# A graph network on one core: the edge softmax moves into the first aggregation

## The reference

```
h   = relu(layernorm(x))
el  = sum_f((h @ W_src + b_src)[n, head, f] * attn_l)      # 8 heads of 64 features
er  = sum_f((h @ W_dst + b_dst)[n, head, f] * attn_r)
V   = h @ W_val + b_val
e   = leaky_relu(el[src] + er[dst], 0.2)                   # one score per edge and head
w   = exp(e - segment_max(e, dst)[dst])
x   = x + segment_sum(V[src] * w / segment_sum(w, dst)[dst], dst)
h   = relu(layernorm(x))
for W, b in ((W1, b1), (W2, b2)):                          # two GCN layers
    h = relu(D^-1/2 (A + 2I) D^-1/2 (h @ W) + b)
x   = x + h
```

## Time and profile before

| | us |
|---|---|
| median of three runs | 4095.23 |
| the profiled execution | 4099.47 |
| its span in the trace | 4097.7 |
| start to first gather of V rows | 688.6 |
| first aggregation | 688.6 to 1680.1 |
| residual, LayerNorm, W1 | 1680 to 1888 |
| first GCN aggregation, W2, second one | 1888 to 4097.7 |

### The profile page before, as it was taken

How to read it: one execution, slowest core, us unless ns; L and a number is a source line. 1 busy time by engine, 2 the same in 40 slices (tenths; PEclk the granted TensorE clock), 3 DMA queues, 4 the chain that set the end, 5 groups by cost and what they waited for, 6 DMA issues and landing times.

```text
span 4097.7 us, 54022 instructions
## 1 busy us (share of the span) xinstructions
PE 3458.8 (84%) x14584; PEld 1665.2 (41%) x14584; DVE 2264.1 (55%) x3817; ACT 1782.7 (44%) x4149; POOL 2664.8 (65%) x2781
## 2 busy tenths in 40 slices
PE   6999987777788888897788888898996888888887
PEld 4699943222233333343333333333442333333333
DVE  7699886777788888883222333333552222323336
ACT  6266513444445555454333444444343333434442
POOL 3776402777777777655777777777007777777775
PEclk9999998999999999998999999999998899999998
DMA  8532336777777777556777777777117777777779
GB/s 317 153 68 62 86 108 215 210 210 209 210 210 210 210 210 210 189 203 192 210 210 209 210 210 210 209 210 210 56 67 231 209 210 210 210 210 210 210 208 355
DMA packets 313528, 794.46 MB, mean 194 GB/s; under 512 B 73690, under 2 KB 97388, under 8 KB 312282
## 3 DMA queue, kind: packets, MB, share of 16 engines
q0 software_dynamic: 201216, 630.92, 52.8%
q1 hardware_dynamic: 84845, 111.13, 8.3%
q10 hardware_dynamic: 27276, 50.30, 3.5%
HBM read 708.94 MB, written 84.00 MB: 194 GB/s over the span
## 4 chain that ended last, share of the span: by engine, by line
PE 31%; POOL 25%; issue 21%; DMA 13%; DVE 8%; POOLq 1%; ACT 1%; DVEq 1%; ACTq 0%; SPq 0%
POOL edge L1302 19%; PE mm L1555 8%; DMA rows_wmat<-v_tab,src_group 6%; POOL rows_wmat L1302 5%; DMA edge<-h_tab,src_group 5%; PE sm L1726 4%; PE mm L1654 4%; PE tr L1654 4%; PE mm L1726 3%; DVE edge L887 2%; PE tr L1726 1%; PE sm L1599 1%; PE tr L1550 1%; PE hist_ps L1726 1%; PE misc L1726 1%
## 5 line engine op out<-in xcount | busy, mean ns | idle before, releaser
L1302 POOL DMA_INDIRECT edge<-h_tab,src_group x1564 | 1489.6, 952 | 708.1 <-issue 448.5
L1462 ACT ACTIVATE hots<-iota,drel 128x128 f32<-128x128 f32 x1760 | 538.0, 388 | 1179.1 <-PE tr L1726 616.6
L1302 POOL DMA_INDIRECT rows_wmat<-v_tab,src_group x782 | 741.5, 948 | 282.5 <-issue 213.4
L1726 PE MATMUL mm<-edge,hots 128*128 x880 | 457.9, 669 | 206.0 <-SPq L1118 204.8
L1726 PE MATMUL sm<-edge,hots 128*128 x880 | 451.6, 661 | 141.8 <-SPq L1118 138.2
L912 DVE TENSOR_TENSOR big<-big,mm 128x512 f32 x220 | 151.3, 688 | 698.9 <-PE tr L1726 680.6
L912 DVE TENSOR_TENSOR big<-big,sm 128x512 f32 x220 | 151.3, 688 | 601.6 <-PE misc L1726 587.6
L1726 PE MATMUL tr<-edge,hots 128*128 x880 | 395.6, 592 | 0.0
L1726 PEld LDWEIGHTS mm<-edge,hots 128*128 128x128 f32 x880 | 179.8, 212 | 478.3 <-issue 478.2
L1555 PE MATMUL mm<-rows_wmat 128*128 128x512 f32 x784 | 354.9, 596 | 0.0
L1726 PEld LDWEIGHTS sm<-edge,hots 128*128 128x128 f32 x880 | 179.7, 211 | 405.3 <-issue 405.0
(11 more groups left out here) (254 smaller groups left out, 4470.8 us busy)
## 6 DMA issues: line engine op xcount, KB each, us to landing
h_tab<-rows_wmat SPq DMA_DIRECT2D x98, 256.0 KB, 2.0
edge<-h_tab,src_group POOLq DMA_INDIRECT x1564, 3.7
rows_wmat<-low_tab SPq DMA_DIRECT2D x145, 128.0 KB
v_tab<-rows_wmat ACTq DMA_DIRECT2D x49, 256.0 KB, 2.9
x_tab<-big SPq DMA_DIRECT2D x49, 256.0 KB, 2.1
rows_wmat<-v_tab,src_group POOLq DMA_INDIRECT x782, 3.7
edge<-x SPq DMA_DIRECT2D x48, 256.0 KB
out<-big ACTq DMA_DIRECT2D x48, 256.0 KB
```

Source lines behind the costliest of these rows:

```text
L1302: pool.indirect_dma_start(ring[:, 2 * u + c, :], None, tab, bass.IndirectOffsetOnAxis(ap=src_group[:, n:n + 1], axis=0)).then_inc(a["rows_ ...
L1462: act.activation(group_hots[:, q % 2, e, :], iota[:, :], ACT.Abs, bias=drel[:, col:col + 1], scale=-1.0).then_inc(a["dist_set"], 1)
L1726: last = pe.matmul(agg_ps[bank][:, :], group_hots[:, q % 2, w % GROUP * 2 + n, :], edge[:, ds(slot[w % OFFS] + n * D, D)], start=(n == 0), ...
```

## The change

**Scores inside the aggregation.** A row of `v_tab` grows from 512 to 528 floats: for each head 64 values and a constant one (520, `AS`), then the node's eight `el`. The fetched row so brings `el[src]`, and the ones make the aggregation sum the weights themselves: the accumulator is 49 tiles of 520 columns. `el_tab`, `low_tab`, `w_tab`, `sum_tab`, the lookups (lines 1654, 1261), the scans over all edges, the transposes of the weights and the gathers of denominators (1312) go. `ht_tab` goes as well: `h` stays in SBUF.

**Turns.** The first aggregation has 440 static steps in 55 turns of 8 steps, or 16 chunks. Two chunks are fetched for every step, 880 in all, at fixed places of a ring of 32 chunks (two turns); GpSimd asks for free places four chunks at a time. No table of positions is read in it. In the last four steps of a turn the next turn's weights are made: ScalarE copies the 16 chunks' `el` to one 128x128 tile (`take_el`), TensorE transposes it so that a partition is one (chunk, head) pair and the 128 edges lie along the free axis; VectorE adds `er`, applies the leaky ReLU and runs a maximum scan backwards and forwards; the ends of the 16 chunks go through a small matmul, are scanned for carries on eight partitions, go back through a second one, and are applied; then ScalarE's exponential and a transpose back. The maximum is only over the edges up to this turn, so at the start of the next turn the accumulator of the tile in work is multiplied by exp(old - new maximum).

**Preparation.** New DRAM tables: `around_rows` (each group with its neighbour edges), `er_rows`, `mask_rows`. GpSimd gathers 4 blocks of `around_rows`, 4 of `src_rows`, 4 first `er` and 4 of `er_tab` rows (8192 bytes each row). VectorE makes masks and spreads `er` in 4 blocks of 128 steps; SyncE stores both, and then loads 3 small pieces per turn.

**Steps' shape.** Messages are 128x1040 instead of 128x1024. TensorE writes two halves of 260 columns, so four matmuls per step where there were two. Three message buffers instead of five, accumulation two steps behind instead of four, four one-hot pairs instead of eight, three pairs of PSUM banks instead of six banks. The GCN stages keep their 782 gathers.

```diff
+AS = D + H
+RW = AS + H
+TURN = 8
+STEPS = TURNS * TURN
+ROWS_AHEAD = 32
+PIECE = 4
-MSGS = 5
-BEHIND = 4
+MSGS = 3
+GAT_HOTS = 4
+BEHIND = 2
...
 VectorE
+            def spread_er(b):
+                dve.wait_ge(er_in[b % 2], 16 * (b // 2 + 1))
+                if b == 0:
+                    dve.wait_ge(er_first_in, 16 * blocks)
+                else:
+                    dve.wait_ge(er_rows_kept, 32 * b)
...
+                for h in range(H):
+                    issue(dve.tensor_tensor_scan(er_out[:, h, :], cont[:, b, 0:GE], got[:, :, h], er_carry[:, b, h:h + 1],
+                                                 ALU.mult, ALU.add))
...
+            def scores(b):
+                bank = turn_ps[b % 2]
+                dve.wait_ge(scored, b + 1)
+                dve.wait_ge(turn_in, 48 * (b + 1))
+                turn_did(dve.tensor_tensor(score, bank[:, 0:P], turn_er, ALU.add))
+                turn_did(dve.scalar_tensor_tensor(score, score, SLOPE, score, ALU.mult, ALU.max))
+                turn_did(dve.tensor_tensor_scan(back[:, ::-1], turn_pen[:, 1:P + 1][:, ::-1], score[:, ::-1], -BIG,
+                                                ALU.add, ALU.max))
+                turn_did(dve.tensor_tensor_scan(fore, turn_pen[:, 0:P], back, -BIG, ALU.add, ALU.max))
+                turn_did(dve.tensor_tensor(spread, fore[:, 0:P:P - 1].unsqueeze(2).to_broadcast([P, 2, 2 * TURN]),
+                                           chunk_of.unsqueeze(1).to_broadcast([P, 2, 2 * TURN]), ALU.mult))
+            def carries(b):
...
+                dve.wait_ge(heads_sum, b + 1)
+                turn_issue(dve.tensor_copy(now[:, 0:1], old[:, n:n + 1]))
+                turn_issue(dve.tensor_tensor_scan(now[:, 1:n + 1], ...
+                turn_issue(dve.tensor_tensor_scan(now[:, n + 1:2 * n + 1][:, ::-1], ...
+            def arguments(b):
...
+                dve.wait_ge(carries_sum, b + 1)
+                for s in range(2):
+                    turn_issue(dve.scalar_tensor_tensor(spread[:, s, :], bank[:, at:at + n], 1.0, chunk_of, ...
+                                                        accum_out=carried[:, s:s + 1]))
+                turn_did(dve.scalar_tensor_tensor(back, pen_head, carried[:, 0:1], fore, ALU.add, ALU.max))
+                turn_did(dve.scalar_tensor_tensor(fore, pen_tail, carried[:, 1:2], back, ALU.add, ALU.max))
+                turn_issue(dve.tensor_scalar(shrink, fore[0:H, 0:1], now[:, 0:1], 0.0, ALU.subtract, ALU.max))
+                turn_issue(dve.tensor_tensor(score, score, fore, ALU.subtract))
...
             def aggregate_weighted(a):
+                        if b + 1 < TURNS:
+                            if j == TURN - 3:
+                                scores(b + 1)
+                            if j == TURN - 2:
+                                carries(b + 1)
+                            if j == TURN - 1:
+                                arguments(b + 1)
+                        if j == 0:
+                            dve.wait_ge(w_turned, b + 1)
+                        if k >= MSGS:
+                            dve.wait_ge(a["step_sum"], k - MSGS + 1)
...
+                        if w % TURN == 0 and w:
+                            dve.wait_ge(shrink_sum, w // TURN)
...
+                            dve.scalar_tensor_tensor(tile, ..., 1.0, tile, ALU.add, ALU.mult).then_inc(shrunk, 1)
...
 GpSimd
-            gather(v_tab, agg[0], gat_ring, msg_set)
+            for n in range(2 * STEPS):
+                if n % PIECE == 0 and n >= ROWS_AHEAD:
+                    wait_alone("pool", pool, gat["msg_set"], (n - ROWS_AHEAD + PIECE) // 2)
+                pool.indirect_dma_start(ring[:, n % ROWS_AHEAD, :], None, v_tab, bass.IndirectOffsetOnAxis(
+                    ap=src_step[:, n:n + 1], axis=0)).then_inc(gat_rows_in[n // PIECE % PIECES], 16)
...
 TensorE
+                    if b + 1 < TURNS:
+                        for at, stage in enumerate((score, carries, carries_out, weights)):
+                            if j == TURN - 4 + at:
+                                stage(b + 1)
...
+                    for c in range(2):
+                        for half in range(2):
+                            last = pe.matmul(gat_ps[k % 3][:, half, :], onehot[:, k % GAT_HOTS, c, :],
+                                             msgs[:, k % MSGS, c, half * (AS // 2):(half + 1) * (AS // 2)],
+                                             start=(c == 0), stop=(c == 1))
...
 ScalarE
+                    if n % TURN == 0 and n:
+                        weights(n // TURN)
+                    if n % TURN == TURN - 4 and n // TURN + 1 < TURNS:
+                        take_el(n // TURN + 1)
...
 SyncE
+            for b in range(TURNS):
+                n = 2 * TURN
+                if b:
+                    sp.wait_ge(turn_set, marks[f"arguments{b - 1}"])
+                turn_of = mask_chunks[b * n:(b + 1) * n, :]
+                sp.dma_start(turn_masks, turn_of.unsqueeze(1).to_broadcast([n, H, MASKS])).then_inc(turn_in, 16)
+                sp.dma_start(turn_er, er_lines[b * P:(b + 1) * P, :]).then_inc(turn_in, 16)
+                    sp.dma_start(chunk_masks, turn_of[:, 2 * P:2 * P + 2].unsqueeze(0).to_broadcast([H, n, 2])).then_inc(turn_in, 16)
...
+            sp.wait_ge(gat["step_sum"], STEPS)
             load_tabs()
```

More of the change, by code:

```diff
@@ L799, in _ @@
[L799 to L802 removed]
+            for b in range(2):
+                make_masks(b)
+            for i in range(len(turns)):
+                take_turned(i)
+                if i + 2 < len(turns):
+                    settle()
+                    to_turn(i + 2)
+                if i < 2:
+                    make_masks(i + 2)
             settle()
             marks["tables"] = prep[0]
[L805 to L806 removed]
@@ L822, in _ @@
-            carries(back_local, True)
-            for half, at in enumerate(halves):
-                did(dve.tensor_tensor(el[:, at, :], el[:, at, :], top[:, at, :], ALU.subtract))
-                marks[f"arg{half}"] = prep[0]
+            for b in range(blocks):
+                spread_er(b)
+            dve.wait_ge(er_zeroed, 16)
+            did(dve.tensor_reduce(head_of, ident[:, :].rearrange("p (c h) -> p h c", h=H), AX.X, ALU.add))
+            did(dve.tensor_reduce(chunk_of, ident[:, :].rearrange("p (c h) -> p c h", h=H), AX.X, ALU.add))
@@ L1130, in _ @@
-            pipelined(sp, PCOLS // Q, 4, 0, load_low, tail=PCOLS // Q - ER_LOAD)
-            with nc.allow_non_contiguous_dma(reason="one step of the tables per partition"):
-                sp.dma_start(need_tab.rearrange("b p -> p b"), need_i[:, :]).then_inc(tabs_kept, 16)
-                for n in range(2):
-                    sp.dma_start(slot_tab[n].rearrange("b p -> p b"), slotcol_i[n][:, :]).then_inc(tabs_kept, 16)
-            all_landed(sp, el_in, GCOLS)
-            load_tabs()
-            by_part = w_tab.rearrange("g n -> (g n)").rearrange("(p n) -> p n", p=P)
@@ L1423, in _ @@
[L1423 to L1436 removed]
+            act.wait_ge(h_turned, TILES)
@@ new lines, in take_el, with weights @@
+            def take_el(b):
+                half, n = b % 2, 2 * TURN
+                for piece in range(PIECES // 2):
+                    act.wait_ge(gat_rows_in[half * (PIECES // 2) + piece], 16 * PIECE * (b // 2 + 1))
+                if b:
+                    act.wait_ge(turn_set, marks[f"arguments{b - 1}"])
+                act.activation(fore.rearrange("p (c h) -> p c h", h=H), ring[:, half * n:(half + 1) * n, AS:RW],
+                               ACT.Copy).then_inc(el_set, 1)
+            def weights(b):
+                act.wait_ge(turn_set, marks[f"arguments{b}"])
+                act.activation(back, score, ACT.Exp).then_inc(w_exp, 1)
+                if b:
+                    act.wait_ge(shrink_turned, b)
+                    if b >= 2:
+                        act.wait_ge(shrink_sum, b - 1)
+                    act.activation(grown, turn_ps[b % 2][0:1, P + 4 * 2 * TURN:P + 4 * 2 * TURN + H], ACT.Exp,
+                                   scale=-1.0).then_inc(shrink_set, 1)
@@ new lines, in _ @@
+            turns = [4] * blocks + [min(4, CHUNK_BLOCKS - b) for b in range(0, CHUNK_BLOCKS, 4)]
+            for i, n in enumerate(turns):
+                pe.wait_ge(dve_prep, marks[f"block{i}"])
+                for k in range(n):
+                    last = pe.transpose(tr[i % 2][:, k * P:(k + 1) * P], b_f[:, i % 2, k * P:(k + 1) * P], ident[:, :])
+                last.then_inc(pe_prep, 1)
+                values(1)
+            values(TILES - values_done[0])
+            pe.wait_ge(v_set, TILES)
```

1008 lines of the change are left out of this document (363 added, 645 removed).

## The result

The changed kernel takes 3871.3 us (median of 4 runs, 3866.9 to 3875.3) against 4095.1 beside it: a ratio of 0.945, interval 0.944 to 0.947, 224 us faster. The forecast was 3896, with 3850 to 3975 as its range.

A forecast was written before the change was run, and what follows sets the result against it. GpSimd's gathers pace the first aggregation, behind a 688.55 us preparation chain. From 4099.5 us profiled: start -381.5, aggregation +141.0, sharing +38.5, residual +3 give 3900.5; less 4.2 for the median, 3896 us, range 3850 to 3975.

The forecast's parts named there:

- GpSimd paces, 880 gathers: First aggregation: GpSimd sets the pace; 880 gathers at 1.253 us make 1101.5 us against 978.7, +122.7.
- rival 4: Aggregation gathers: longer rows slow them, by length (35 us; 3893 or 3931; chance 0.03) or second descriptor (4271; 0.01).
- Sharing, +38.5: First aggregation: VectorE operations with two SBUF inputs slow GpSimd's gathers, 0.7 us a turn over 55 turns, +38.5 us.
- rival 2: Aggregation: a turn's dependencies pace, or GpSimd stands still 2.2 us; turn 21.5 to 23 us, 3938 to 4020; chance 0.18.
- Start, 307: Before the aggregation: V's last store starts the gathers of V rows at 307 instead of 688.55 us, -381.5 us.
- (a): Preparation, V: eleven tiles by 167.25, six transposed blocks with a tile each until 192, 32 more until 303, landed 307.
- (b): Preparation, `er`: scatters, gathers, then four rounds of eight scans at 11.5 us each, ending at 293, ahead of V.
- VectorE, 18.3 to 19, and the turn's chain: Aggregation: VectorE needs 18.3 to 19 us of a 20.05 us turn; the chain for next weights leaves 1.5 us.
- The tail of 31 us and the residual's +3: Behind the last issued V gather 31 us, before 12.8; residual stage +3 us, SyncE's three table loads preceding x and W1.
- Rivals 3 and 5: Aggregation turn with exposed trips and landing, 25.7 us, 4169, chance 0.05; start set by `er` chain at 345, 3934, 0.06.
- rival 1: Aggregation: GpSimd keeps 1.253 us a gather although VectorE reads SBUF twice; 3858 us; chance 0.15.
- the forecast's own case: Whole kernel: GpSimd paces, slowed by sharing, start set by V; 3896 us, this case ranging 3875 to 3925; chance 0.52.

The follow-up runs named there:

- the runs with short and long operations: Changed kernel plus, per GCN accumulation, four 120-column additions (3944.1 us) or one 480-column addition (3925.9 us), both inputs in SBUF; changed kernel 3877.9 us.

## Why the prediction was right, and where it was not

**GpSimd paces, 880 gathers.** Right: +126.0 us from first to last gather, of which +122.7 are the 98 extra gathers at the old pitch. The longer rows cost nothing: the median gather is 946 ns (949 in another execution), against 949 before, so rival 4 is out. Its landing is 3.8 against 3.7.

**Sharing, +38.5.** This term failed: it was 33.1 us too high, more than the whole error of 25 us, from which the late start below took some back. The forecast took a rate from 6.5 us of growth beside 24.0 us of line 1010 and multiplied it by 2.2 us a turn. Of that growth 5.2 us stand beside line 1010; the rest, 1.3, stands beside the one-tile multiplication of line 1001. In the changed kernel 880 gathers grew by 837.9 - 880 x 0.946 = 5.4 us. The rows had the right law in them: in the earlier trace rows the operation ends at 4056.02, the gather started at 4055.43, and 4056.02 - 4055.43 - 0.12 = 0.47, just the growth, and all 17 gathers that started so within line 1010 keep it within 0.02 us. So a gather is held by an operation that is running at its start, until 0.12 us before that operation's recorded end. What the gather itself keeps VectorE from is short: an operation that starts with it waits 0.04 us, and one that starts 0.04 us or more behind it, not at all. At a random phase an operation of length L so costs (L - 0.12)^2/2.5: 0.13 us at 0.69, but 0.04 at a scan's 0.42 and 0.01 at 0.29. The seven operations of a turn, 0.20 to 0.43 us long, make 0.14 us, 8 us over 55 turns. Measured are 5.4, of which 4.1 stand beside the one pair that has no gap in it, line 737 and the subtraction behind it: 20 gathers started in the former and were held until 0.12 us before the end of the latter, 1.15 us or so each. One turn's scores, with gathers among them:

```profile
919.95 0.29 DVE L706 TENSOR_TENSOR work<-misc,work 128x128 f32<-128x128 f32 x1 [1.61 <-PE misc L1456]
920.27 0.34 DVE L707 SCALAR_TENSOR_TENSOR work<-work 128x128 f32<-128x128 f32 x1
920.28 0.95 POOL L1166 DMA_INDIRECT work<-v_tab,src_flat  x1 [0.30 <-issue]
920.64 0.42 DVE L708 TENSOR_TENSOR_SCAN work<-work 128x128 f32<-128x128 f32 x1
921.10 0.43 DVE L710 TENSOR_TENSOR_SCAN work<-work 128x128 f32<-128x128 f32 x1
921.53 0.95 POOL L1166 DMA_INDIRECT work<-v_tab,src_flat  x1 [0.30 <-issue]
```

The scan of 0.42 started 0.36 us after the gather and the next one ended at 921.53, as a gather started; neither held one. (The gather at 920.28 started 0.01 us into line 707, which took 0.34 us in place of its usual 0.29.) The standstill of rival 2 is refuted too, by the runs with short and long operations: 970 us of such work made the gathers 19 us longer.
The Trainium skill (SBUF — State Buffer, "Who interferes with whom") is borne out in which operations interfere (two SBUF inputs yes, one in PSUM no) and in that the lock is exclusive. What this case adds is that a gather keeps VectorE waiting for only some 0.04 of its 0.95 us.

**Start, 307.** It came at 314.3. The step that failed is in (a), where the six blocks' transpositions follow the eleventh tile without a wait. TensorE stood idle for 7.84 us ahead of the first, since the gathers of destinations, which these blocks are made of, landed after 10.1 us. The forecast allowed for a queue only in (b). Most of that wait is due to the two stores of 4-byte pieces, which the change had moved from 503 us to 162: with them elsewhere it was 0.99 us, and the first gather came 5.0 us earlier. The V tiles went at 3.43 us (113.32 for 33), against 3.48. Chain (b) ended at 293.4, when SyncE, which waits for its last store, went on to the turns' loads; the forecast had 293. VectorE's rounds started 11 to 16 us apart, where 11.5 was forecast.

**VectorE, 18.3 to 19, and the turn's chain.** Right: 18.27 us a turn when it sets the pace, and GpSimd's waits for it are 7.6 us in all. TensorE's records of 260 columns have a median of 0.382 (mean 0.391), as forecast.

**The tail of 31 us and the residual's +3.** Right: 30.8 and 2.9.

With the sharing term at its measured 5.4 and the start at 314.3 the sum is 3900.5 - 33.1 + 7.3 = 3874.7 for the profiled execution; the rest, some 6 us, is the GCN stages' 3.3, 2.1 in the aggregation and small differences.

**Rivals 3 and 5** didn't come about; rival 1, GpSimd unhindered at 3858, is nearer to the truth than the forecast's own case, in its mechanism and in its number. The measured 3871.3 lies below the 3875 to 3925 of the forecast's own case, and in the whole range because that made room for rival 1, to which 0.15 was given. That the error is 25 us and not 33 is luck: two errors with opposite signs.

## What to carry to other kernels

Contention between two engines is priced by the moment at which one needs what the other holds, so read single pairs of rows (start, start, end) before taking a rate from sums: the rate made 38.5 us out of 5.4, while one pair of rows held the law that the later pairs bore out. Short operations beside GpSimd's gathers are nearly free, long ones with both inputs in SBUF are not, and neither is the one-tile multiplication of line 1001. When a change moves small stores, look at what stands in the DMA queues at their new place: 1024 pieces of 4 bytes tripled the landing of gathers on the critical chain.

## What the runs showed of the hardware that was not expected

- A GpSimd indirect DMA (0.946 us) is held by a VectorE operation with two SBUF inputs if it starts 0.03 us or more into it, and grows by what is left of it less 0.12 us: 135 of 138, 393 of 401 and 17 of 17 gathers within 0.02 us. A multiplication of one tile in SBUF by a value per partition (128x512, 0.48 us) holds it too: 15 of 15. With one input in PSUM: 1.1 us of growth over 447 gathers.
- The other way round the hold is short: an addition that starts with a gather takes 0.69 us in place of 0.65, one that starts 0.04 us behind it 0.65.
- A gather that nothing holds takes 0.946 us in some executions of the same kernel and 0.949 in others.
- The starts of the two engines kept a common phase in the GCN stages, and the number of collisions (138) is far from that of a random phase (370).
- Packets of 4128 bytes that started at 164 to 168 us, beside or just behind some 1100 packets of 4 bytes, took 1.5 to 2.0 us in the mean of each of six profiles, and 0.21 and 0.24 us in the two without them; the gathers landed after 10.1 to 10.6 us and after 2.9.
